# GpSimd's scatters and gathers inside the experts, released by VectorE's product instead of TensorE's step

## The reference

```
gates = jax.nn.softmax(x @ wg.T, axis=-1)          # 2048 tokens, 64 experts
w_topk, idx_topk = jax.lax.top_k(gates, 8)         # eight experts for each token
buf = zeros((64, 160, 128)).at[se, rank].set(x[st])  # up to 160 tokens per expert
h = jnp.einsum('ech,efh->ecf', buf, expert_w1)     # 128 -> 768
x1, x2 = jnp.split(h, 2, axis=-1)
out = jnp.einsum('ecf,ehf->ech', x1 * jax.nn.silu(x2), expert_w2)   # 384 -> 128
y = out[se, rank] * sw                             # gate of the token
combined = zeros((2048, 128)).at[st].add(y)
```

## Time and profile before

| | us |
|---|---|
| median of 3 runs (lowest, highest) | 718.93 (718.65, 720.97) |
| the profiled execution's own time | 723.01 |
| its span from first to last instruction | 721.2 |
| PE busy | 580.0 (80%) |
| DVE busy | 453.1 (63%) |
| POOL busy | 345.1 (48%) |
| ACT busy | 230.2 (32%) |

### The profile page before, as it was taken

How to read it: one execution, slowest core, us unless ns; L and a number is a source line. 1 busy time by engine, 2 the same in 40 slices (tenths; PEclk the granted TensorE clock), 3 DMA queues, 4 the chain that set the end, 5 groups by cost and what they waited for, 6 DMA issues and landing times.

```text
span 721.2 us, 11097 instructions
## 1 busy us (share of the span) xinstructions
PE 580.0 (80%) x3755; PEld 479.8 (67%) x3755; DVE 453.1 (63%) x1362; ACT 230.2 (32%) x434; POOL 345.1 (48%) x341
## 2 busy tenths in 40 slices
PE   7998878668987787797999035789999999999960
PEld 5767655668977776797995024567787778778640
DVE  4678768943424322333433787887877787777994
ACT  3142234002322212222332011224344444443664
POOL 4656101873566666576444488343322332342352
PEclk9999997879999999999999556799999999999995
DMA  8960001126666766676716900000000000000001
GB/s 298 415 260 23 16 7 36 45 72 203 209 222 200 231 220 190 190 237 218 239 61 213 398 2 0 0 12 5 15 26 4 15 15 11 4 30 0 1 1 59
DMA packets 29564, 79.42 MB, mean 110 GB/s; under 512 B 7104, under 2 KB 12096, under 8 KB 29264
## 3 DMA queue, kind: packets, MB, share of 16 engines
q1 hardware_dynamic: 23088, 65.69, 26.3%
q0 software_dynamic: 6432, 13.16, 6.0%
HBM read 62.60 MB, written 16.25 MB: 109 GB/s over the span
## 4 chain that ended last, share of the span: by engine, by line
PE 58%; DVE 23%; issue 8%; another core or an unknown queue 4%; POOL 2%; ACT 2%; DMA 1%; SPq 0%; DVEq 0%; ACTq 0%; POOLq 0%
PE bank L780 13%; PE bank L946 6%; PE bank L790 6%; PE bank L934 6%; PE bank L539 4%; PE bank L876 3%; PE bank L894 2%; DVE stats L256 2%; DVE arena L1659 2%; PE bank L857 2%; PE bank L871 2%; DVE hidden L1743 2%; PE bank L885 2%; PE bank L912 2%
## 5 line engine op out<-in xcount | busy, mean ns | idle before, releaser
L271 POOL TENSOR_TENSOR rstd<-veps,minus_half 128x4 f32<-128x4 f32 x52 | 54.0, 1039 | 209.9 <-DVE veps L264 208.4
L780 PE MATMUL bank<-hidden,ring 128*128 128x160 f32 x768 | 123.4, 311 | 4.6 <-issue 2.7
L780 PEld LDWEIGHTS bank<-hidden,ring 128*128 128x128 f32 x768 | 113.4, 200 | 6.5 <-issue 4.3
L1347 POOL DMA_INDIRECT returned_rows<-x1t,scatter_all x80 | 79.3, 991 | 65.9 <-DVE x1t L1754 21.8
L1153 ACT ACTIVATE hidden<-bank 128x480 f32<-128x480 f32 x64 | 36.9, 576 | 177.6 <-PE bank L780 110.5
L790 PE MATMUL bank<-hidden,ring 128*128 128x160 f32 x384 | 66.4, 310 | 31.8 <-DVE hidden L1743 19.1
L790 PEld LDWEIGHTS bank<-hidden,ring 128*128 128x128 f32 x384 | 56.0, 193 | 37.3 <-DVE hidden L1743 22.8
L1731 DVE COPY hidden<-bank 128x384 f32<-128x384 f32 (+1 forms) x32 | 22.9, 719 | 66.3 <-PE bank L780 33.9
L1211 ACT ACTIVATE arena<-bank,layer_cols 128x512 f32<-128x512 f32 x64 | 44.0, 687 | 62.6 <-PE bank L934 62.6
L946 PE MATMUL bank<-ring,arena 128*128 128x128 f32 x512 | 59.9, 275 | 1.4 <-issue 1.4
L946 PEld LDWEIGHTS bank<-ring,arena 128*128 128x128 f32 x512 | 58.4, 192 | 2.4 <-issue 2.4
(11 more groups left out here) (222 smaller groups left out, 1156.9 us busy)
## 6 DMA issues: line engine op xcount, KB each, us to landing
ring<-in_ew SPq DMA_DIRECT2D x64, 576.0 KB
returned_rows<-zeros SPq DMA_DIRECT2D x16, 512.0 KB, 14.6
arena<-returned_rows SPq DMA_DIRECT2D x6, 512.0 KB, 12.7
hidden<-returned_rows SPq DMA_DIRECT2D x4, 512.0 KB, 5.0
ring<-returned_rows SPq DMA_DIRECT2D x4, 512.0 KB, 8.6
ring<-in_l1w SPq DMA_DIRECT2D x8, 256.0 KB, 2.6
returned_rows<-x1t,scatter_all POOLq DMA_INDIRECT x80
shared<-in_xr SPq DMA_DIRECT2D x1, 1024.0 KB, 8.3
```

Source lines behind the costliest of these rows:

```text
L271: pool.tensor_tensor(rstd[:, s, :], veps[:, s, :], minus_half[:], ALU.pow).then_inc(sem(f"rstd{which}_ready"), 1)
L780: mm = pe.matmul(bank[2 * (n % 2) + part][:, CAP * f:CAP * f + CAP], ring[:, n % RING, P * (FB * part + f):P * (FB * part + f) + P], E["xt ...
L1347: pool.indirect_dma_start(returned_dram[:, :], bass.IndirectOffsetOnAxis(ap=scatter_all[:, Q, b:b + 1], axis=0), E["back"][:, Q % BACK, b, ...
```

## The change

One line of `step`. Each portion of GpSimd now waits for VectorE's product of the step instead of TensorE's `expert_mm`, and the cap is 64 instead of 66. No instruction is added, removed or put in another order on any engine; the waits for `back_read`, `slot_gate_ready`, `indices_ready` and `zeroed` stay.

```
             def step(n):
-                pool.wait_ge(sem("expert_mm"), min(n + 1, NE + LAG))
+                pool.wait_ge(sem("prod_g_ready"), min(n + 1, NE))
```

## The result

| | before | after |
|---|---|---|
| median of 5 runs (lowest, highest), us | 720.97 (718.65, 722.42) | 733.44 (727.75, 735.21) |
| the profiled execution's own time, us | 723.01 | 727.75 |
| its span, us | 721.2 | 726.0 |

Ratio 1.0178 [1.0148, 1.0208], +12.5 us; the forecast was no change. The profiled execution of after is the quickest of its five, so the two profiles differ by 4.8 us only: what follows shows where the time went, and less of it than the median has.

A forecast was written before the change was run, and what follows sets the result against it. TensorE (PE) was taken as the bound, losing 3 to 4 us a quad to late signals where GpSimd gathers. Steady state 0 plus 0.6 us at the end, on the median 718.93, gave 719.5 us, range 711 to 730.

The forecast's parts named there:

- So in steady state the sum is 0: Experts' gather stretch: portions start 1.3 us later, but GpSimd's 2.4 us of waiting a quad absorbs it; 0 us.
- The slower rival: Gather stretch: late signals hang on GpSimd's block of eight DMAs, so each quad's loop grows 1.3 us; +12 us, chance 0.33.
- my whole reading fails: Failure sign: stalls move to other steps with another size, so the gathers' place against the steps decides, not the waits' length.
- The argument I had against it: Against the slower rival: at 162.76 a signal came 4.0 us late with gathers still to start.
- The faster rival: Gather stretch: scatters of j = 0 no longer meet the step of j = 1; 13 us at most, 705 us, chance 0.24.
- The end: Last ten scatters: the first waits for product 64 instead of expert_mm 65, delaying everything behind; +0.62 us.
- What the prediction put at 0 in the scatter stretch: Where GpSimd only scatters: first portion moves behind the product, under 1.3 us, with 4.55 us idle ahead; 0 us.
- The rule on the VectorE port: Copy-like VectorE instructions lock GpSimd out of its descriptor ports; separation worth 1.9 us at most, none on the path.
- That a matmul's end is estimated: TensorE's late signals may be work inside its array, since matmul ends aren't observed; none of the terms depends on it.

The follow-up runs named there:

- e12: The kernel before with GpSimd's step wait removed altogether, on a 721 us chip: 727.57 us, ratio 1.0097.
- e15: The kernel before with only GpSimd's scatter portions waiting for the product, gathers still for expert_mm, on a 721 us chip: 733.08 us, ratio 1.0147.
- e13: The kernel before with the scatters of quads 0 to 12 left out, on a 721 us chip: 679.46 us.
- e14: The kernel before with the gathers of quads 6 to 15 left out, on a 721 us chip: 681.60 us.
- e3_tail_only: The kernel before with only the portions of steps 64 and later waiting for the product, on a 678 us chip: 677.70 us, ratio 0.9991.
- e8: The kernel before, with TensorE at j = 0 of quads 3 to 12 also waiting for quad Q+3's gathered rows: 770.82 us, ratio 1.0706.
- e9: The changed kernel, with TensorE at j = 0 of quads 3 to 12 also waiting for quad Q+3's gathered rows: 780.03 us, ratio 1.0803.

## Why the prediction was wrong

**The step that failed** is "So in steady state the sum is 0". It was worked out from slack: GpSimd is ready 2.4 us before the next signal, so 1.3 us more is absorbed. That holds only if the signal keeps its time. It doesn't: on this chip the signals that are delayed longest come 1.3 to 1.9 us behind the end of GpSimd's run (246.98 behind 245.67, 262.08 behind 260.24 in before; 254.92 behind 253.13 in after; 1.7 us in e12 and e15). That holds for all 26 signals over 4.6 us late from 190 to 345 us in these four traces. It doesn't hold for those of 2 to 4.5 us: some pass amid a run (257.01 in before, 3.0 us late), some within 0.2 us of its end (242.58) or 0.6 us behind it (239.09 in after). What I called slack was GpSimd waiting for something that waited for GpSimd. A later start gives a later end, and so a later signal.

**The slower rival came true** by its mechanism. That its 12 us are so near the measured 12.5 is in part luck, since the parts differ. Its loop, which I had read in one quad and given a third, closes in e12 and e15 to a tenth of a microsecond, with two lengths of the same link. Two things in it were wrong. First, the size a quad: not 1.3 us each, but 1.3 us for two quads in the regular part, and the rest where single quads became long ones (two of 11.9 and 11.8 us in before take 16.4 and 14.3 in after, one of 15.6 takes 20.1). I had read the regular stretch of before, with its 15.2 us, as the whole; its ten quads take 11.8 to 17.1 us. A scatter starts 0.8 us behind a product, a gather 0.26 us. Where the late signal of before was answered by a scatter (0.74 us behind it) and that of after by a gather (254.92 to 256.45, 1.53 us), the link grew by 0.8 us and not by 1.3. Second, it isn't the eight DMAs of one place that count: the stalls moved from j = 0 and 1 to j = 3 and 2. I had written that my whole reading fails in that case, and it did.

**The argument I had against it**, the early signal with gathers still to start, misled me. The same step on a 678 us chip is not late, so the earlier trace rows was a case of the same effect, not evidence against it: signals that pass amid a run occur in the loop as well.

**The faster rival** fell: moving the scatters off the step at j = 1 freed that step and stalled others.

**The end** was right in its wait: +0.61 us for +0.62. What the prediction put at 0 in the scatter stretch was not: with the five scatters of the last such quad released later, the last signal is 1.1 us later behind its matmuls than in before, and that is on the path. No run takes this piece apart by itself. **The rule on the VectorE port** would have made it a gain. Scatters take 0.99 us on average before and after, so the change gained nothing by it. The rows that the prediction compared don't test it well: two scatters stand amid a product, though the rule as told is one of copies, and at 387.98 VectorE is not idle as I wrote, its line 1791 runs to 388.12. Better ones in before say the same: a scatter with VectorE idle throughout (250.29) takes 0.98 us, and one with a copy of line 1731 inside it (247.72, the copy from 248.21) takes 0.98 us too.

**That a matmul's end is estimated** (the Trainium skill, Perfetto Trace Analysis, "Tensor Engine Instruction") left open whether the array or the signal is late. e13 and e14 show that the array does the same work without a gap when GpSimd's DMAs are thinned out. The recorded starts from 250.19 to 254.11 show that in some stalls matmuls of the next step are held up as well; in others they are not (the twelve from 239.82 in before start within 1.79 us, and VectorE gets their signal 5.4 us late). Whether the awaited step's own matmuls are held up, no run shows. Open too is why GpSimd's runs make TensorE's signals late, and why on some chips only.

## What to carry to other kernels

Slack that is measured as "engine A waits for B's signal" is worth nothing until it is shown that the signal doesn't depend on A; where a loop closes to a tenth in the trace, price it as a loop, and compare the links that each variant puts in. When a signal comes later than the work behind it explains, and ends its lateness a fixed time behind another engine's run, suspect that engine in the loop, even if no semaphore says so, and thin its work out to see. And look where the waiting goes when a wait is removed: here another dependence on the same late signal took its place.

## What the runs showed of the hardware

- The same kernel takes 678 us on four of the chips that the experiments ran on and 721 us on two others, the same in every run on one chip. Whether it is the chip or where the program lies in its memory, no run tells. All 43 us lie in the experts: in e3_tail_only the adding behind them starts at 354.92 us, in before at 398.00, and PE is busy 137.82 of 140 us against 111.84.
- On the slower kind TensorE's step signals come up to 8.0 us late (332.00 in after) while GpSimd's indirect DMAs run long without a pause, and those delayed longest pass 1.3 to 1.9 us behind the end of the run. With one kind left out, and so with runs of five at most, a signal is 2.5 us late at most in the loop (e13, e14), and TensorE has 1 us of gaps in 140 or none.
- A run of gathers has landed 1.7 to 1.9 us behind the end of GpSimd's work on it (e8, e9).
- An indirect DMA of 128 rows in the experts' loop occupies GpSimd 0.94 to 1.02 us with a gap of 0.30 us, the same on both kinds of chip. Behind the loop one takes 1.19 us in before (380.05) and 1.26 us in after (385.17), both beside VectorE's line 1787.
